# First attention on four parts of the PE array, and four successive rows in one partition

## The reference

```
x = x + xattn0(layernorm(x), ctx)      # 16 heads, 77 keys; the feature map is exp(z), exp(-z) of 8 -> 8
x = x + ffn0(layernorm(x))             # 8 experts of 64 hidden, the 2 best weighted, and a shared one
x = x + xattn1(layernorm(x), ctx, mask)  # one head of 128, 77 keys, masked
x = x + ffn1(layernorm(x))             # 8 experts of 512 hidden, the 2 best of each token
```

## Time and profile before

| | us |
|---|---|
| median of 3 runs | 459.58 |
| span of the profiled execution (no time is listed for it apart from its span; the three runs are 459.45 to 460.05) | 460.0 |
| setup of the first attention, up to the first score matmul | 60.7 |
| its main loop, up to the first matmul of the first FFN | 60.7 to 171.7 |
| PE busy / DVE / ACT / POOL over the span | 372.7 / 252.0 / 150.5 / 175.7 |
| span left after the last expert matmul (438.3) | 21.7 |

### The profile page before, as it was taken

One profiled execution on the slowest core, in us unless ns is written; L12 is line 12 of the kernel. 1 busy time (PEld: TensorE's weight loads), 2 busy tenths in 40 slices (PEclk: granted clock), 3 DMA queues, 4 the chain that ended last, 5 costly groups with the idle time before them and its releaser, 6 DMA issues.

```text
span 460.0 us, 6601 instructions
## 1 busy us (share of the span) xinstructions
PE 372.7 (81%) x2130; PEld 290.7 (63%) x2131; DVE 252.0 (55%) x708; ACT 150.5 (33%) x267; POOL 175.7 (38%) x211
## 2 busy tenths in 40 slices
PE   3851879999999999699999598414999999999910
PEld 2421758787887884356558487402788888888800
DVE  5999633426465045551353979588355454545414
ACT  2462522323323225221121556110244343444413
POOL 5999980001010010400111511325466666666322
PEclk9987779999899599655999979655799999999965
DMA  5500000000000001500000444100111111112064
GB/s 146 119 1 0 2 0 1 0 1 0 1 2 0 1 0 41 166 1 0 2 0 1 137 118 135 46 1 13 29 47 51 42 49 43 48 43 48 23 171 120
DMA packets 29352, 18.97 MB, mean 41 GB/s; under 512 B 6683, under 2 KB 27055, under 8 KB 29327
## 3 DMA queue, kind: packets, MB, share of 16 engines
q1 hardware_dynamic: 26831, 13.53, 10.6%
q0 software_dynamic: 2496, 5.12, 4.0%
HBM read 13.99 MB, written 4.65 MB: 41 GB/s over the span
## 4 chain that ended last, share of the span: by engine, by line
PE 68%; DVE 23%; DMA 2%; issue 2%; POOL 2%; ACT 1%; SPq 1%; DVEq 0%; ACTq 0%; POOLq 0%
PE ps L1150 58%; PE ps L1573 4%; DVE xn L556 3%; DVE kbhi L624 3%; DVE qlo L630 3%; DVE stats L544 2%; PE ps L1322 1%; DMA dnT<-y_dram 1%; DVE uplo L797 1%; PE ps L1548 1%; DVE x L806 1%; PE ps L1279 1%; DVE mv L547 1%; PE ps L1450 1%; DVE x L962 1%
## 5 line engine op out<-in xcount | busy, mean ns | idle before, releaser
L390 POOL TENSOR_SCALAR rstd<-mv 128x4 f32<-128x4 f32 x16 | 4.0, 251 | 200.6 <-DVE mv L547 200.6
L504 POOL DMA_INDIRECT y_dram<-yb,dst_row x39 | 38.4, 984 | 33.4 <-DVE yb L937 33.4
L640 DVE TENSOR_REDUCE mx<-ps 128x8 f32<-128x616 f32 x32 | 25.6, 799 | 46.3 <-PE ps L1150 46.0
L1042 ACT ACTIVATE ex<-ps 128x512 f32<-128x512 f32 (+1 forms) x40 | 23.9, 597 | 76.4 <-PE ps L1150 76.4
L498 POOL DMA_INDIRECT xg<-xn_dram,src_row x39 | 37.9, 972 | 16.5 <-PE ps L1548 9.3
L1150 PEld LDWEIGHTS ps<-Vx,ex 128*128 128x128 f32 (+1 forms) x320 | 41.7, 201 | 0.9
L1150 PE MATMUL ps<-dnT,hhT 128*128 x312 | 41.4, 276 | 0.6 <-DVE yb L937 0.6
L1150 PE MATMUL ps<-Vx,ex 128*128 128x51 f32 (+2 forms) x320 | 41.5, 278 | 0.0
L1150 PEld LDWEIGHTS ps<-dnT,hhT 128*128 128x128 f32 x312 | 37.9, 192 | 4.1 <-issue 0.8
L1118 ACT ACTIVATE gl<-ps 128x512 f32<-128x512 f32 x39 | 23.3, 597 | 47.0 <-PE ps L1150 47.0
L1150 PE MATMUL ps<-uphi,xghi 128*128 x78 | 35.2, 451 | 0.9 <-DVE xghi L923 0.6
(11 more groups left out here) (262 smaller groups left out, 786.7 us busy)
## 6 DMA issues: line engine op xcount, KB each, us to landing
upn<-in_L_ffn_gate_up_w_dram SPq DMA_DIRECT2D x8, 512.0 KB, 4.2
dnn<-in_L_ffn_down_w_dram SPq DMA_DIRECT2D x8, 256.0 KB, 4.9
dnT<-y_dram SPq DMA_DIRECT2D x8, 256.0 KB, 4.9
x<-in_x_dram SPq DMA_DIRECT2D x4, 256.0 KB, 3.7
xn_dram<-xn SPq DMA_DIRECT2D x4, 256.0 KB, 2.3
out_dram<-x SPq DMA_DIRECT2D x4, 256.0 KB, 2.3
xg<-xn_dram,src_row POOLq DMA_INDIRECT x39, 2.5
y_dram<-yb,dst_row POOLq DMA_INDIRECT x39, 2.2
```

The lines of the kernel that those rows point to most:

```text
L504: g.indirect_dma_start(y_dram, bass.IndirectOffsetOnAxis(ap=dst_row[:, k:k + 1], axis=0), yb[:, k % 2, :], None).then_inc(scattered[k % 2] ...
L640: v.tensor_reduce(mx[:, b % 2, i, half * HH:half * HH + HH].rearrange("p (a h) -> p a h", a=2), ps[:, pair:pair + 2, 0:HK // 2].rearrange( ...
L1042: s.activation(ex[0:rows, m % RING, :], bank[1 + m % 2][0:rows, :], ACT.Exp, scale=SCALE).then_inc(act_ex, 1)
```

## The change

1. **Layout.** `pack0`, `pack1`, `pack2` and the turned context are made before launch from the inputs; three DMAs take the place of 14 small ones, and the turning of context and weights by PE falls away.
2. **Four heads at a time.** The 16 heads are 4 groups of 4; head j of a group has partitions 32j to 32j+31 (16 features and, in row 32j+16, the negated maximum). Products over 32 rows are issued as four matmuls at partitions 0, 32, 64 and 96, to banks 0 to 3 (`spread`, `scores`); products with 32 output rows as four matmuls to partitions 0, 32, 64, 96 of bank 6 (`values`). All these are plain fp32; the hi/lo split of q and k, `sel` and `nmT` are gone.
3. **The maximum.** 16 `max_job`s a batch, each one fp32r matmul of 308 columns on the full array, each with one DVE reduction of 308 columns. The maxima are turned as fp32, copied negated by ACT (`copy_mT`) and brought to row 32j+16 by four DMAs a batch on SP's queue, each 4 rows of 2 KB.
4. **16 steps instead of 40.** A step G is `scores(G)`, some max jobs, `values(G-1)`, `turn_values(G-2)`, the other max jobs. ACT takes two exps of 77 x 1024 a step and copies `oT`.
5. **Rows.** Partition p holds tokens 4p to 4p+3 of a batch in x, mask and output, and `xn_dram` and `y_dram` are laid out so that a partition's run is 2 KB; the index arithmetic for gather and scatter follows. y is read back by 4 DMAs of 512 KB, and DVE does the last addition for all four batches.
6. **Moved.** Folding the second attention's weights goes from the setup to the last four steps and one after, with its copies from ACT to DVE. `attention_out(b)` moves from a batch later to two batches later; the gates of batches 0 and 1 are done in the last batch's steps and behind them; normalised x of batches 2 and 3 is turned in the FFN.

```diff
+            def spread(src, cols, n):
+                for g in range(NG):
+                    ins = mm(bank[g][:, 0:n], Wz[R * g:R * g + R, :], src[R * g:R * g + R, cols])
+                return ins
...
+            def scores(G):
+                b, g = divmod(G, NG)
+                pe.wait_ge(shifted[b % 2][g], 16 * (b // 2 + 1))
+                if G >= 1:
+                    pe.wait_ge(act_ex, 2 * G)
                 else:
+                    pe.wait_ge(act_qs, NG * NB)
+                for j in range(GH):
+                    rows = slice(R * j, R * j + FD + 1)
+                    ins = mm(bank[j][0:KEYS, :], kst[rows, g, b * KEYS:(b + 1) * KEYS], qs[rows, b, g, :])
+                    if j % 2:
+                        ins.then_inc(pe_sc, 1)
...
+                for j in range(GH):
+                    ins = mm(bank[6][R * j:R * j + R, :], Vx[:, b, g * P + R * j:g * P + R * j + R],
+                             ex[:, (2 * G + j // 2) % RING, j % 2, :])
+                ins.then_inc(pe_av, 1)
...
+                if k >= 2:
+                    pe.wait_ge(dve_max, k - 1)
+                mm(bank[4 + n % 2][:, 0:GK], qh[:, b % 2, g, i * P:(i + 1) * P], kb[:, b, g, :]).then_inc(pe_max, 1)
...
+            for b in range(NB):
+                sp.wait_ge(act_mT, b + 1)
+                for g in range(NG):
+                    sp.dma_start(qs[FD:P:R, b, g, :], mT[GH * g:GH * g + GH, b % 2, :]).then_inc(shifted[b % 2][g], 16)
...
+            for G in range(STEPS + 2):
+                b, g = divmod(G, NG)
+                if G < STEPS:
+                    scores(G)
+                if b + 1 < NB:
+                    for n in range(MAX_SPLIT[g][0], MAX_SPLIT[g][1]):
+                        max_job(b + 1, n)
+                if 1 <= G <= STEPS:
+                    values(G - 1)
+                if G >= 2:
+                    turn_values(G - 2)
+                if b + 1 < NB:
+                    for n in range(MAX_SPLIT[g][1], MAX_SPLIT[g][2]):
+                        max_job(b + 1, n)
+                    if g == 2:
+                        turn_max(b + 1)
...
-        x_dram = A["x"].rearrange("b (i p) d -> b p i d", p=P)
+        x_dram = A["x"].rearrange("b (p i) d -> b p i d", p=P)
...
-                for c in range(CH):
-                    sp.dma_start(yc[:, b, c, :, :],
-                                 y_dram[c * ROWS + b * SEQ:c * ROWS + (b + 1) * SEQ, :].rearrange("(i p) d -> p i d", p=P))\
-                        .then_inc(y_loaded[b], 16)
+                sp.dma_start(yc[:, b, :, :, :], y_rows[:, :, b * NI:(b + 1) * NI, :]).then_inc(y_loaded[b], 16)
```

More of the change, by code:

```diff
@@ L21 @@
 HEADS, HD, FD = 16, 8, 16
[L22 to L24 removed]
+GH = 4
+NG = HEADS // GH
+GK = GH * KEYS
+R = P // GH
 E0, H0 = 8, 64
@@ L440, in _ @@
+            layernorm_rstd(0, 0)
+            layernorm_rstd(0, 1)
+            g.wait_ge(act_kst, NG)
+            spread_keys(1)
+            layernorm_rstd(0, 2)
+            round_queries(1)
+            layernorm_rstd(0, 3)
+            for b in range(2, NB):
+                spread_keys(b)
+            round_queries(2)
             add_bias(0)
@@ L737, in _ @@
-            normalise(NB - 1, UNIT_GROUPS[2:])
+            v.wait_ge(ld_l0, 16)
+            v.tensor_tensor(bz[:, :], fmb, sgn, ALU.mult).then_inc(dve_bz, 1)
+            for b in range(2):
+                v.wait_ge(ld_x[b], 32 if b == 0 else 16)
+                layernorm_stats(b)
+            layernorm_apply(0, 0)
+            v.wait_ge(act_kst, NG)
+            v.tensor_tensor(kb[:, 0, :, :].bitcast(F32R).rearrange("p g (j k) -> p g j k", j=GH),
+                            wide(kst[:, :, 0:KEYS].unsqueeze(2), P, NG, GH, KEYS),
+                            wide(maskJ[:, :].unsqueeze(1).unsqueeze(3), P, NG, GH, KEYS), ALU.mult).then_inc(dve_kb, 1)
@@ new lines, in queries, with copy_mT, copy_oT @@
+            def queries(b, dst, signal):
+                s.wait_ge(pe_z, b + 1)
+                for g in range(NG):
+                    s.activation(dst[:, g, :], bank[g], ACT.Exp, bias=bz[:, 0:1], scale=sgn).then_inc(signal, 1)
+            def copy_mT(b):
+                s.wait_ge(pe_nmT, b + 1)
+                s.activation(mT[:, b % 2, :], bank[4][0:HEADS, :], ACT.Copy, scale=-1.0).then_inc(act_mT, 1)
+            def copy_oT(G):
+                s.wait_ge(pe_av, G + 1)
+                if G >= 2:
+                    s.wait_ge(pe_T, G - 1)
+                s.activation(oT[:, G % 2, :], bank[6], ACT.Copy).then_inc(act_oT, 1)
@@ L1026, in copy_onT @@
                 s.activation(onT[:, 2 * pair:2 * pair + 2, :, :].rearrange("p i a t -> p (i a t)"),
-                             bank[0], ACT.Copy).then_inc(act_onT, 2)
+                             bank[7 if b < NB - 1 else 0], ACT.Copy).then_inc(act_onT, 2)
+            copy_xT(0, 0, bank[0])
+            queries(0, qh[:, 0], act_qh)
+            queries(0, qs[:, 0], act_qs)
+            copy_xT(0, 1, bank[6])
+            queries(1, qs[:, 1], act_qs)
+            copy_xT(0, 2, bank[7])
+            queries(2, qs[:, 2], act_qs)
@@ L1255, in gate_logits, with turn_on @@
-            def gate_logits(b, last):
+                    ins = pe.transpose(bank[7][:, i * P:(i + 1) * P], oT[:, G % 2, i * P:(i + 1) * P], ident[:, :])
+                ins.then_inc(pe_T, 1)
+            def turn_on(b, pair, dst):
+                for i in range(2):
+                    for a in range(2):
+                        at = (2 * i + a) * P
+                        ins = pe.transpose(dst[:, at:at + P], on[:, b % 2, 2 * pair + i, a * P:(a + 1) * P], ident[:, :])
+                ins.then_inc(pe_onT, 2)
@@ L1256, in gate_logits, with project @@
+            def project(b, dst):
+                pe.wait_ge(ld_w, 16)
+                pe.wait_ge(act_onT, (b + 1) * NI)
+                for i in range(NI):
+                    for a in range(2):
+                        ins = mm(dst[:, i * D:(i + 1) * D], onT[:, i, a, :], fcT[:, a, :], a == 0, a == 1)
+                ins.then_inc(pe_fc, 1)
+            def gate_logits(b, last, dst):
                 pe.wait_ge(ld_small, 16 * N_SMALL)
@@ new lines, in _ @@
+            transpose_xn(0, 0, bank[0])
+            queries(0)
+            pe.wait_ge(act_vx, 3)
+            transpose_xn(0, 1, bank[6])
+            queries(1)
+            for n in range(HEADS // 2):
+                max_job(0, n)
+            for n in range(HEADS // 2, HEADS):
+                max_job(0, n)
+            turn_max(0)
+            pe.wait_ge(act_vx, NB)
+            transpose_xn(0, 2, bank[7])
+            queries(2)
+            pe.wait_ge(xT_ready, 2)
+            transpose_xn(0, 3, bank[6])
```

826 lines of the change are left out of this document (332 added, 494 removed).

## The result

The changed kernel takes 468.20 us (median of 4 runs, 465.21 to 469.00), the kernel before 459.81 on the same chip (4 runs, 459.45 to 460.05). The ratio is 1.0175, with a 95% interval of 1.0133 to 1.0218. Forecast was 438, faster. The profiled execution took 468.95 and its span is 466.4, against 460.0 before.

| stage | before | forecast | after |
|---|---|---|---|
| start to first score matmul | 60.7 | 44.4 | 52.9 |
| to the first matmul of the first FFN | 111.0 | 102.7, and 4 for the clock | 130.2 |
| to the issue of the last scatter of y | 267.3 | 269.8 | 266.4 |
| to the end | 21.1 | 17.4 | 17.0 |

A forecast was written before the change was run, and what follows sets the result against it. Setup was taken as bound by DVE (60.7 us), the loop by PE (111.0), the end by y read back, added and stored. 460.0 - 16.3 - 8.3 + 2.5 - 3.7 + 4 = 438.2, so 438; range 418 to 476.

The forecast's parts named there:

- Price of the four-part matmuls: Main loop, `scores` and `values`: each taken as three records, 1.3 us, between bounds of 0.86 and 3.44.
- The main rival: `scores` and `values`: record order lets only neighbouring parts overlap, five records, 2.15 us each, 464 in all; chance 0.33.
- q: Time of one `scores` or `values`: four fp32 matmuls in four array parts, eight records; taken as 1.3 us.
- Clock, "+4": Main loop: lower clock level costs 4 us, half of the 9 it was worth in the old loop.
- the lower clock for the whole loop: Main loop: at half the clock it ends at 222 instead of 147, about 510 us; chance 0.12, shared with no overlap.
- Loop at the upper clock, 102.7: Main loop, priced at the upper clock throughout: 102.7 us instead of 111.0, a term of -8.3.
- Setup, -16.3: Start to first score matmul: at 44.4 us instead of 60.7, without `kbhi`, `qlo`, `kblo` and the turning of weights.
- the normalisation of batch 2 while POOL rounds queries, 3.0: Setup, behind the max jobs: DVE normalises batch 2 beside POOL's rounding of queries, priced at 3.0 us.
- First FFN, +2.5: First FFN: DVE has a normalisation (1.1) and half a gate chain (2.6) more before the gates' copy; bounds 0 and +5.
- two chains of 4.8: Main loop: moved gates, two chains of small DVE instructions before the reads of the folds, 9.6 us together.
- End, -3.7: After the last scatter: reading y saves at most 1, DVE is quicker without POOL beside it; bounds 0 and -6.

The follow-up runs named there:

- the trace with zeros: Changed kernel with 32 rows instead of 17 named in each score matmul, the 15 added holding practically zeros: 439.85 us, ratio 0.9742 to the kernel before.
- Undoing the contention: Changed kernel with POOL's spreading of keys of batches 2 and 3 waiting until DVE has normalised all batches: 475.68 us, ratio 1.0213 to the kernel before.

## Why the prediction was wrong

- **Price of the four-part matmuls: right, and better than taken.** 1.02 us at the upper clock instead of 1.3. (The 0.43 for a record's stream stands in no row of before, where starts are 0.24 apart for fp32r and 0.48 for fp32; in the trace with zeros four fp32 records start 0.43 apart, 156.0 to 157.3.) The main rival, parts serialised by the order of their records (q = 2.15), is refuted: the four parts' first records start together. The sign of the result agrees with that rival, its reason doesn't.
- **Clock, "+4": the step that failed.** I took the share of the lower clock from the old loop (18 of 111 us) and halved it, arguing that fewer short matmuls would keep the clock up. What the runs showed in its place: with 17 rows a part the lower level holds from the setup to about 154 us but for some 3 us, though PE is 81 to 96% busy; with 32 rows, in the same order of instructions, it ends 23 to 43 us into the loop. The difference is 27 us (130.2 - 103.0), where the term had 4. The fact that 17 of 128 rows hold anything stood among the rivals ("the lower clock for the whole loop", chance 0.12) and was outvoted by "most of the old loop ran at 0.9 or more". That rival's price was too high in turn: it has 178 us for a loop at the lower clock (222 - 44), and 130.2 were measured with all but some 20 us of it there. That q was 1.0 and that waits for DVE and ACT don't grow with the clock would explain it; neither was priced apart.
- **Loop at the upper clock, 102.7: right in sum, by two errors.** With zeros in the rows it is 103.0. It holds some 20 us at the lower clock, which the 102.7 didn't have. A q of 1.0 instead of 1.3 pays for it: 32 times 0.28 is 9 us, about what 23 us at half the clock lose at most (11.5). Both are estimates.
- **Setup, -16.3: right in kind, half in size, -7.8.** `kbhi`, `qlo` and `kblo` are gone as written. The 8.5 us between 44.4 and 52.9: the queries of batch 1 start at 22.4 and not at 19.5 (2.9; 1.28 of it is ACT's table load in front of the first exp, left out of my sum, and 1.4 the 16 turned tiles, which take 3.25 from 10.42 to 13.67 instead of 1.8); at the lower clock, 0.51 from 20 to 50, they take 2.1 instead of 1.5 (0.6); the 16 max jobs take 10.8 (24.5 to 35.3) instead of 9.3 (1.5), a pair 1.2; and from there to the first score matmul it is 17.6 instead of 14.1 (3.5), with the end of batch 3's normalisation on the path. That is the mis-sized term, "the normalisation of batch 2 while POOL rounds queries, 3.0": batch 2's took 1.11, but batch 3's 7.50, beside POOL's products (2.2 each, which were taken as hidden). Undoing the contention brought the first score matmul 2.6 us forward by itself and 5.1 together with 32 rows.
- **First FFN, +2.5: -0.9**, 0.9 below its lower bound of 0; the stage was not taken apart, and the traces differ in the clock there, so the cause stays open. The moved gates, priced inside the loop at two chains of 4.8, cost somewhat more: between the last `values` (170.1) and the first FFN matmul (183.0) one chain takes 5.4 on DVE, from 169.6 to 174.9, with one of its instructions long beside POOL's mask addition:

```profile
169.51 2.58 POOL L401 TENSOR_TENSOR mask_i<-mask_i,keyc 128x1232 f32<-128x1232 f32 x1 [10.72 <-DVE keyc L560]
...
169.79 2.36 DVE L506 TENSOR_TENSOR r_b<-r_a,r_m 128x32 f32<-128x32 f32 x1
```

- **End, -3.7: -4.1, right in size, wrong in place.** I gave all of it to reading y (less 1) and to DVE alone without POOL (less 2.7). The additions are only 1.3 nearer to the last scatter, because y lands later than thought (DVE starts 4.4 us after SP's first issue, 3.8 before) and DVE is then the bound for four batches. The other 2.8 lie after the last addition, where nothing was forecast.
- **The range held by luck.** 468 lies inside 418 to 476, but in the part that was there for the serialised records (452 to 478), which did not happen. The case that did, the lower clock for nearly the whole loop, was named as left out of the range.

The estimate by the Trainium skill (TensorE: Matmul & The Clock Gate, "Part 3: Packing small matmuls", 3.07 times for four row parts, q = 1.12) lies nearer to the 1.02 measured than mine; here it is 3.44 / 1.02 = 3.4 times.

## What to carry to other kernels

Price a matmul that uses part of the array at both clock levels, and give the lower one a real chance even where PE will be nearly always busy: here it was worth 27 us, more than setup and end gave together (11.9). Where the operands have room, try letting such a matmul name the whole of its part: here rows of zeros left the shortest and the longest matmul as they were, and the upper clock that lasted came at 76 us instead of 154. And when an edit takes DVE work out of a setup, look at what POOL then does beside the DVE instruction that is late next.

## What the runs showed of the hardware

- Four fp32 matmuls of two records each, in four row parts, take 1.02 us at the upper clock, against 0.86 priced for one; so do four column parts (1.00).
- 17 named rows a part: lower clock for about 100 us on end (22 to 123 us); 32 with zeros: upper clock from 76 us on. With the full-array fillers, 16 in the setup and 30 in the loop, it came at 128.
- DVE's `xn` of four tiles: 1.11 us alone, 7.50 beside POOL's products, cast and additions. A small `r_b` of 32 columns: 0.19 alone, 2.36 beside POOL.
- The clock column and the speed of the rows can differ: 1.00 beside records at the lower level's duration, from 54 to 76 us in one trace of 32 rows, and in the changed kernel from 10 to 14 us, where turned tiles take 417 ns (421 at 0.50 and 272 at 1.00 later on). Trust starts and durations.
- What made the lower level last 23 us of the loop in some runs with 32 rows and 43 in another was not found out, nor why the last store ends 2.8 us sooner with the new layout, whose runs are of 2 KB.
